# A decoder layer on one core: two data exchanges made inside SBUF, and the decay tables' sums and steps dealt anew among VectorE, TensorE and GpSimd

## The reference

```python
K = 2.0 * real(einsum('hn,hnl->hl', Ct, exp(dtA[:, :, None] * l)))   # 256 channels, 64 modes, 1024 taps
y = irfft(rfft(x, n=2048) * rfft(K, n=2048).T)[:, :1024]             # long convolution
r = x + y + x * D;  x = layernorm(x + layernorm(r) * ln_w + ln_b)
x = layernorm(x + cross_attention(x, ctx))                           # 16 heads, 77 keys
x = layernorm(x + mlp(x) + experts(x))                               # 1024 hidden, top-k of 1024 experts
```

## Time and profile before

| quantity | us |
|---|---|
| median of 3 runs | 710.08 |
| the three runs | 712.31, 710.08, 703.44 |
| the profiled execution | 702.58 |
| its span, first to last instruction | 700.8 |
| VectorE busy | 506.6 |
| TensorE busy | 590.3 |
| ScalarE busy | 404.9 |
| GpSimd busy | 279.9 |

### The profile page before, as it was taken

One profiled execution on the slowest core, in us unless ns is written; L12 is line 12 of the kernel. 1 busy time (PEld: TensorE's weight loads), 2 busy tenths in 40 slices (PEclk: granted clock), 3 DMA queues, 4 the chain that ended last, 5 costly groups with the idle time before them and its releaser, 6 DMA issues.

```text
span 700.8 us, 9712 instructions
## 1 busy us (share of the span) xinstructions
PE 590.3 (84%) x3132; PEld 383.4 (55%) x3132; DVE 506.6 (72%) x1046; ACT 404.9 (58%) x593; POOL 279.9 (40%) x333
## 2 busy tenths in 40 slices
PE   5743587785296778999999999999999999899996
PEld 2512366563264554445678565478575479453485
DVE  7999985523047885898866879767778797578783
ACT  4971655222042435797763878675579765577760
POOL 0002871635041345543343634235635234644361
PEclk9876989898596567999999999999999999999999
DMA  8945030456325000000000000000000000000000
GB/s 239 363 204 91 1 98 2 119 162 144 89 83 217 1 1 1 0 1 0 1 1 0 17 8 7 1 1 1 9 8 8 8 1 1 8 16 7 0 8 23
DMA packets 20111, 34.27 MB, mean 49 GB/s; under 512 B 7388, under 2 KB 14045, under 8 KB 18333
## 3 DMA queue, kind: packets, MB, share of 16 engines
q1 hardware_dynamic: 15677, 29.46, 13.7%
q10 hardware_dynamic: 4384, 4.20, 2.0%
HBM read 21.94 MB, written 10.65 MB: 47 GB/s over the span
## 4 chain that ended last, share of the span: by engine, by line
PE 60%; DVE 22%; ACT 7%; issue 6%; POOL 3%; DMA 1%; SPq 0%; ACTq 0%; DVEq 0%; POOLq 0%
PE banks L773 20%; PE banks L863 8%; PE banks L868 7%; PE banks L818 4%; PE banks L840 3%; PE banks L795 3%; PE banks L830 3%; PE banks L804 2%; PE banks L715 2%; DVE stats L1377 2%; ACT arena L882 2%; PE banks L651 2%; DVE arena L1468 2%; PE banks L855 2%; ACT arena L1067 1%
## 5 line engine op out<-in xcount | busy, mean ns | idle before, releaser
L1169 POOL TENSOR_TENSOR arena<-arena 128x1024 f32<-128x1024 f32 x64 | 125.8, 1965 | 156.6 <-ACT arena L1067 155.6
L773 PE MATMUL banks<-arena 128*128 128x512 f32 x384 | 174.6, 596 | 5.4 <-issue 3.7
L773 PEld LDWEIGHTS banks<-arena 128*128 128x128 f32 x384 | 69.9, 190 | 83.2 <-issue 76.5
L1067 ACT ACTIVATE arena<-arena 128x1024 f32<-128x1024 f32 x64 | 73.5, 1149 | 7.5 <-DVE arena L1466 3.2
L1069 ACT ACTIVATE arena<-arena 128x1024 f32<-128x1024 f32 x64 | 73.5, 1149 | 2.1
L1468 DVE SCALAR_TENSOR_TENSOR arena<-arena 128x1024 f32<-128x1024 f32 x48 | 63.8, 1329 | 1.7
L863 PE MATMUL banks<-arena 128*128 128x256 f32 x256 | 58.4, 381 | 2.4 <-DVE tok L1504 1.2
L957 ACT COPY arena<-banks 128x512 f32<-128x512 f32 (+1 forms) x64 | 34.1, 532 | 44.8 <-PE banks L765 29.3
L868 PE MATMUL banks<-arena 128*128 128x256 f32 x256 | 57.9, 379 | 0.0
L1142 POOL TENSOR_SCALAR arena<-mv 128x1 f32<-128x1 f32 (+1 forms) x40 | 14.1, 353 | 105.2 <-DVE mv L1378 103.8
L971 ACT ACTIVATE tok<-tok,arena,rstd 128x256 f32<-128x256 f32 x48 | 27.9, 598 | 45.5 <-POOL arena L1147 44.6
(11 more groups left out here) (179 smaller groups left out, 1077.4 us busy)
## 6 DMA issues: line engine op xcount, KB each, us to landing
scr_x<-arena SPq DMA_DIRECT2D x16, 256.0 KB, 3.2
arena<-scr_x SPq DMA_DIRECT2D x2, 2048.0 KB, 13.8
arena<-scr_z SPq DMA_DIRECT2D x32, 128.0 KB
scr_z<-arena ACTq DMA_DIRECT2D x14, 256.0 KB, 7.1
tok<-in_x SPq DMA_DIRECT2D x8, 256.0 KB, 5.7
out<-tok SPq DMA_DIRECT2D x16, 128.0 KB, 1.7
arena<-in_imat SPq DMA_DIRECT2D x1, 1152.0 KB, 5.6
arena<-in_fmat SPq DMA_DIRECT2D x1, 1088.0 KB, 7.0
```

Source lines behind the costliest of these rows:

```text
L773: ins = mm(bk[:, :], w[:, k, P * m:P * m + P], src[:, k, :], start=(k == 0), stop=(k == KC - 1))
L1067: fn(ebuf[m % 2], sxb[m % 2], ACT.Prelu, bias=negt[:, n % 2, h:h + 1], alpha=FAR).then_inc(s_ranked, 1)
L1169: tt(sxb[m % 2], sim[:, n % 2, h, 0:XR].unsqueeze(2).broadcast_to((P, XR, NKEYS)), sim[:, n % 2, FH + h, :].unsqueeze(1).broadcast_to((P, ...
```

## The change

- **x**: the 16 stores go straight from `cA` to `xS`, 8 partitions each; `scr_x` and the two loads are gone. `fmat` and one row of biases are loaded earlier. All nine `x_second` come before `taps(0)`, on two pairs of banks, and their evacuations before the taps'. GpSimd's `x_bias` moves ahead of the tables.
- **z**: SyncE's queue waits for each evacuation and moves each plane from `zring` to `zB`; `scr_z`, ScalarE's stores and the loads back are gone. The ring has three slots; `inverse` uses two pairs of banks from its fifth step on.
- **Tables**: VectorE's subtraction is gone. In groups 0 to 3 and 7 TensorE accumulates v's two terms by twice as many matmuls, in groups 4 to 6 GpSimd adds them. Groups alternate between banks 0, 1 and 4, 5.
- **Small steps**: GpSimd makes both `growth` products and half of the mode weights (gains and norms), VectorE's list drops from 28 to 13 steps there. ScalarE takes the exponential first in half 0 and last in half 1, and copies keys (with bias, to `kstage`) and values out of PSUM; the value bias is a matmul. VectorE makes `kbd` only after the tables (`keys`).
- **Numbers** of `PLACE` and `LAG` for the later part shift by thousandths, which exchanges some neighbours in the order.

```diff
--- before.py
+++ after.py
-ZRING = 4
+ZRING = 3
+V_ON_POOL = (4, 5, 6)
+Z_NARROW = 4
...
-         "taps": (0.982,), "x_second": (-0.756, 0.69), "skip": (0.382,), "k_first": (5.96, 0.01, 9.6, 0.059),
-         "simw": (-1.866,), "x_bias": (2.891, 0.086), "values": (2.518,), "diagonal": (-1.627,),
-         "k_second": (7.974, 0.1, 9.65, 0.1), "spectra": (7.989999999999999, 0.1, 9.67, 0.1),
-         "inverse": (8.27, 0.1, 9.9, 0.12), "products": (0.0, 1.0, 0.0, 0.996, 0.0, 0.802, -0.084, 0.975),
...
+         "taps": (0.982,), "x_second": (-2.2, 0.237), "skip": (1.3, 0.3), "k_first": (5.99, 0.66, 9.6, 0.247),
+         "simw": (-2.4,), "x_bias": (-1.5, 0.573), "values": (3.1,), "stage": (-2.527,), "keys": (9.559,),
+         "diagonal": (-1.42,), "k_second": (8.7, 0.13, 10.05, 0.1), "spectra": (9.027, 0.13, 10.11, 0.1),
+         "inverse": (9.076, 0.13, 10.25, 0.11), "products": (0.0, 1.0, 0.0, 0.996, 0.0, 0.802, -0.084, 0.975),
...
-SCRATCH = (("scr_x", (QUAD, 2, 2, NS, NSLOT, B * D)), ("scr_z", (2, NSLOT, P, B * HC)),
-           ("scr_v", (B, HEADS, NKV, HD + 1)))
+SCRATCH = (("scr_v", (B, HEADS, NKV, HD + 1)),)
...
-    imat = imat.reshape(P, FREQ, 2, 2, NQ, NS).transpose(0, 1, 2, 3, 5, 4).reshape(P, FREQ, 2, P)
+    imat = imat.reshape(P, FREQ, 2, 2, NQ, NS).transpose(0, 1, 2, 5, 3, 4).reshape(P, FREQ, 2, P)
...
-        cross_terms = part("cross_terms", o_tab + 4096, 2, CH, HALF)
+        v_terms = [part(f"v_terms{d}", at, 2, CH, HALF) for d, at in enumerate((o_tab + 4096, o_par))]
...
+        def x_bank(m):
+
+            return 4 * (m % 2)
+
+        def group_bank(g):
+
+            return 4 * (g % 2)
+
         def z_bank(m):
 
-            return 2 * (m % 2) if m >= FREQ else 0
+            return 2 * (m % 2) if m >= Z_NARROW else 0
 
...
-            return len(range(d, upto, ZRING))
+            return sum(len(tiles_of(n % FREQ)) for n in range(d, upto, ZRING))
...
+            sp.dma_start(rows[0:1, 4, :], t["rows"][0:1, 4, :]).then_inc(s_ctx, 16)
+            sp.dma_start(fmat, t["fmat"]).then_inc(s_mat, 16)
             sp.dma_start(wqf, t["wqf"]).then_inc(s_wsim_in, 16)
             sp.dma_start(keysT, t["keysT"]).then_inc(s_wsim_in, 16)
 
             for q in range(NQ):
                 sp.wait_ge(s_xae, 2 * (q + 1))
                 for h in range(2):
-                    sp.dma_start(scr_x[q % QUAD, q // QUAD, h].rearrange("s r n -> (s r) n"),
-                                 cA[:, h, q, :]).then_inc(s_xaw, 16)
-            for dst, n in ((rows[:, :, :], "rows"), (head_mask[:, :], "head_mask"), (value_mask, "value_mask")):
+                    p0 = NS * (4 * (q % QUAD) + 2 * (q // QUAD) + h)
+                    sp.dma_start(xS[p0:p0 + NS, 0:NSLOT, :], cA[:, h, q, :]).then_inc(s_xaw, 16)
+            sp.dma_start(rows[:, 0:4, :], t["rows"][:, 0:4, :]).then_inc(s_rows, 16)
+            for dst, n in ((head_mask[:, :], "head_mask"), (value_mask, "value_mask")):
                 sp.dma_start(dst, t[n]).then_inc(s_rows, 16)
-            sp.dma_start(fmat, t["fmat"]).then_inc(s_mat, 16)
-            sp.wait_ge(s_xaw, 16 * 2 * NQ)
-            sp.wait_ge(s_cm, 4)
-            for h in range(2):
-                sp.dma_start(xS[:, 8 * h:8 * h + 8, :].rearrange("p r n -> p (r n)"),
-                             scr_x[:, :, :, :, 8 * h:8 * h + 8, :].rearrange("a b c s r n -> (a b c s) (r n)")).then_inc(
-                                 s_xb[h], 16)
             sp.wait_ge(s_kbz, 1)
             sp.dma_start(t["scr_v"].rearrange("b h k d -> k (b h) d"),
                          vaug.rearrange("k b h d -> k (b h) d")).then_inc(s_vw, 16)
...
+                sp.wait_ge(s_ze, n + 1)
+                for j, r in enumerate(tiles_of(k)):
+                    sp.dma_start(zB[NS * r:NS * r + NS, hf].rearrange("s h q n -> s (h q) n"),
+                                 zring[:, n % ZRING, j, :]).then_inc(s_zw[n % ZRING], 16)
...
-            pe.wait_ge(s_ctx, 16 * 4)
+            pe.wait_ge(s_ctx, 16 * 5)
...
+                    mm(bank[4 + b][0:NKV, D:2 * D], ctxT[:, ic, NKV * b:NKV * b + NKV], wv[:, ic, :],
+                       start=(ic == 0), stop=False)
+                if b == 0:
+                    pe.wait_ge(s_ones, 1)
+                mm(bank[4 + b][0:NKV, D:2 * D], vaug[0:1].rearrange("k b h d -> k (b h d)")[:, 0:NKV], bv[0:1],
+                   start=False, stop=True).then_inc(s_cm, 1)
...
-                if g:
-                    pe.wait_ge(s_kev, 2 * g)
+                if g >= 2:
+                    pe.wait_ge(s_kev, 2 * g - 2)
+                b0 = group_bank(g)
                 v, u = power[g % 2]
+                sums = [(c, table) for c in range(2) for table in ((v,) if g in V_ON_POOL else (v, v_terms[g % 2]))]
+                if g in V_ON_POOL:
+                    pe.wait_ge(s_vtab, V_ON_POOL.index(g) + 1)
                 for k in range(CH // 4):
                     f = slice(4 * k, 4 * k + 4)
                     for half in range(2):
                         modes = slice(64 * half, 64 * half + 64)
-                        for c in range(2):
-                            ins = mm(bank[4 + half][:, P * k:P * k + P], u[modes, c, f, :].rearrange("p f a -> p (f a)"),
-                                     v[modes, c, f, :].rearrange("p f a -> p (f a)"),
-                                     start=(c == 0), stop=(c == 1), skip_group_check=True)
+                        for j, (c, table) in enumerate(sums):
+                            ins = mm(bank[b0 + half][:, P * k:P * k + P], u[modes, c, f, :].rearrange("p f a -> p (f a)"),
+                                     table[modes, c, f, :].rearrange("p f a -> p (f a)"),
+                                     start=(j == 0), stop=(j == len(sums) - 1), skip_group_check=True)
...
-                for h in range(tiles_of(k1)[-1] // 8 + 1):
-                    pe.wait_ge(s_xb[h], 16)
-                if k1:
-                    pe.wait_ge(s_xfe, k1)
-                second_stage(k1, bank[0], bank[1], lambda r: xS[:, r, :]).then_inc(s_xf, 1)
+                pe.wait_ge(s_xaw, 16 * 2 * NQ)
+                b0 = x_bank(k1)
+                if k1 > 1:
+                    pe.wait_ge(s_xfe, k1 - 1)
+                elif k1 == 1:
+                    pe.wait_ge(s_kbz, 1)
+                second_stage(k1, bank[b0], bank[b0 + 1], lambda r: xS[:, r, :]).then_inc(s_xf, 1)
...
+                pe.wait_ge(s_kev, 2 * NGRP - 2)
                 pe.wait_ge(s_yf, m + 1)
-                if m > FREQ:
-                    pe.wait_ge(s_ze, m - 1)
-                elif m:
-                    pe.wait_ge(s_ze, m)
+                if m >= Z_NARROW:
+                    pe.wait_ge(s_tab, NGRP)
+                if m:
+                    pe.wait_ge(s_ze, m - 1 if m > Z_NARROW else m)
...
-                        pe.wait_ge(s_kbd, 1)
                         pe.wait_ge(s_kbz, 1)
+                        pe.wait_ge(s_xfe, FREQ)
...
-                for hf in range(2):
-                    pe.wait_ge(s_zr[hf], 16 * NSLOT)
+                for d in range(ZRING):
+                    pe.wait_ge(s_zw[d], 16 * z_writes(2 * FREQ, d))
...
+                if hf == 0:
+                    own.link(magnitudes())
+                    angles().then_inc(s_sin, 1)
+                else:
+                    own.link(angles())
+                    magnitudes().then_inc(s_sin, 1)
...
+                elif kind == "stage":
+
...
+                    for oc in range(KC):
+                        fn(kstage[:, oc, :], bank[4 + oc][:, 0:B * NKV], ACT.Identity,
+                           bias=pcol[:, 2 + oc:3 + oc]).then_inc(s_kst, 1)
+                        own.done(s_kst)
+                    for b in range(B):
+                        ins = nc.scalar.copy(vaug[:, b, :, 0:HD], bank[4 + b][0:NKV, D:2 * D].rearrange("p (h d) -> p h d", d=HD))
+                        if b == 0:
+                            own.link(ins)
+                        else:
+                            ins.then_inc(s_kbz, 1)
+                            own.done(s_kbz)
...
-                    act.dma_start(scr_z[hf, tiles[0]:tiles[0] + planes].rearrange("r p n -> p r n"),
-                                  zring[:, d, 0:planes]).then_inc(s_zw[d], 16)
...
+            nc.gpsimd.memset(vaug, 1.0).then_inc(s_ones, 1)
+            own.done(s_ones)
...
+            def mode_growth(hf):
+
+                pool.wait_ge(s_phase, hf + 1)
...
+                tt(growth[hf], rates[:, 0:1, f].unsqueeze(3).broadcast_to(full), st, ALU.mult).then_inc(s_growth, 1)
+                own.done(s_growth)
+
+            pool.wait_ge(s_small_ready, 1)
+            own.link(tt(norm, are, are, ALU.mult))
+            own.link(tt(spare, aim, aim, ALU.mult))
+            own.link(tt(norm, norm, spare, ALU.add))
+            nc.gpsimd.tensor_scalar(norm, norm, 0.25, None, ALU.mult).then_inc(s_norm, 1)
+            own.done(s_norm)
+            own.link(tt(gain_re, cre, are, ALU.mult))
+            own.link(tt(spare, cim, aim, ALU.mult))
```

(97 more changed lines are left out.)

94 lines of the change are left out of this document (36 added, 58 removed).

## The result

The changed kernel takes 732.38 us (median of 4 runs, 723.33 to 736.31), the kernel before, beside it on the same chip, 706.76 us (701.15 to 712.31): a ratio of 1.0347, 95% interval 1.0185 to 1.051. It is slower by 3.5%, about 26 us; the interval reaches down to 1.9%: that it is slower is clear of noise, that it is so by over 2% not quite. I had forecast 690, in a range of 669 to 718, and had given 0.17 to anything above 724. The profiled execution of the changed kernel took 731.62 us (span 729.6). Some executions of a kernel are one to two per cent slower than its others, so every ratio here is taken from the fast executions alone.

The account below looks back on a forecast made before the run. Outside TensorE's unchanged last 512.6 us, z's traffic through HBM was taken to bound, with an 18.82 us hole. Conv at 170 instead of 188.2 saves 18 us: 684.5 profiled, plus 5.5 gives 690 us, range 669 to 718.

Parts of the forecast that it names:

- parts 1 and 2: z and x each in one SBUF-to-SBUF hop at 128 GB/s: 33 us for z, 32.8 us for x.
- the row with the same destination: Profile row of the old z loads back from HBM, also writing 8 partitions: 128 GB/s, taken as the moves' rate.
- Part 2 and 3, x: x in place at 54.1 us, then all nine x_second ahead of the tables: taps(0) at 73.7, before 63.89.
- my start of 21.3: Start of the x moves, queued behind all input loads: 18.5 us plus 2.8 us for fmat.
- Part 4, tables: Subtraction gone, VectorE loses 12.5 us, groups of 4.96 us: first inverse at 123 us, before 125.9.
- Parts 1 and 5, z: First inverse to conv: z moves hidden under 42 us of spectra, plus 5 us; conv at 170 instead of 188.2.
- All three signs: Wrong if x_second waits past 65 us (or starts before 45), ScalarE waits over 5 us for slots, taps over 1 us a group for GpSimd.
- the destination is the bound: Rival, 0.14: moves into 8 partitions run near 44 GB/s, 805 us; below 77 GB/s the kernel passes 724.
- Full-speed moves: Rival, 0.19: moves run at 175 to 400 GB/s, x in place by 32 to 45 us, taps(0) about 60; 676 us.
- A compute engine takes the wait: Rival, 0.11: doubled taps at the slow clock, 7.8 us a group, or GpSimd slows; five groups, +14; 704 us.
- The rule's estimate of 771 us: x and z moves into 8 aligned partitions reach two DMA ports, 54 GB/s: 78 us each, 771 us.
- 8 engines: z loads back: DMA share 0.50 with only loads in flight, so they use 8 engines; 286/8 is 35.7 us.

Follow-up runs that it names:

- the spread moves: Changed kernel with x and z moves each writing every 4th partition of a block of 32 instead of 8 neighbours: 675.99 us, 0.9631 of the kernel before.
- x spread: Changed kernel with x moves writing every fourth partition: 699.07 us if only x moves do so, 675.99 us if z moves do too.
- K2 to K4: Move-only batches, SBUF to 8 neighbouring partitions: 1 KB pieces, planes in order; 2 KB pieces in order; planes far apart: 64, 59, 59 GB/s.
- only z spread: Changed kernel with only the z moves writing every fourth partition, x moves keeping 8 neighbours: 711.33 us, 1.0086 of the kernel before.
- z by HBM: Changed kernel with z's exchange alone taken back to scr_z in HBM, ring of three; x moves inside SBUF: 728.25 us, 1.0321 of the kernel before.
- the batch into 16 neighbours: Move-only kernel, no layer computed: 4.19 MB from SBUF in 2 KB pieces into 16 neighbouring partitions: 38.9 us, 108 GB/s.

## Why the prediction was wrong

The step that failed is the choice of one row. In parts 1 and 2 I priced a move into 8 partitions at 128 GB/s, "the row with the same destination". Measured: 69 to 74 GB/s for x, 72 and 47 for z. The profiled execution came out at 731.6 where the sum said 684.5. The 47.1 us divide so:

- **Part 2 and 3, x:** `taps(0)` at 95.9 instead of 73.7, +22.2 us. Only the rate: 4.19 MB at 74 GB/s are 56.7 us, and my start of 21.3 plus that is 78.0; x_second began at 77.3. The nine x_second then took 18.6 us; I had written 18.5 and about 1. (The terms of that 18.5 add up to 19.5, so by them `taps(0)` would stand at 74.6.)
- **Part 4, tables:** 52.1 us instead of 49.3, +2.8 us. No subtraction like that of line 1341 is left, 9.9 of the 12.7 us that I had counted on came through, and `taps` waited for GpSimd 4.3 us in two waits, over the 1 us a group that I had allowed. TensorE's clock was 0.90 there on the mean, not 1.0. 64 records took 5.01 us, not the 4.26 that I made of twice 2.13, and that at a granted clock of 1.00 (106 to 116 us): the step from 32 records to 64 was wrong, not the clock, and why, no run shows. They still fitted the 5.2 us of a group.
- **Parts 1 and 5, z:** first inverse to conv 69.1 us instead of 47, +22.1 us. With the spread moves it took 45.1: here too only the rate was off.
- **Behind conv:** 512.6 us, as forecast.

All three signs that I had named for being wrong are there: x_second waited past 65 us, ScalarE waited 38.7 us for ring slots, and taps waited for GpSimd over 1 us a group.

Of the rivals, "the destination is the bound" (0.14) named the mechanism, the side and the turning point: past 724 us below 77 GB/s. It had only the rate too low (44). With 74 GB/s its working gives x +24 and, at 69.1 us for the whole z stretch, +22: 736. "Full-speed moves" (0.19, 676 us) is what the kernel becomes once the destination is spread: 675.99, with x in place at 42.2 in its 32 to 45 and `taps(0)` at 62.2 in place of its 60. That the medians agree to the microsecond is luck: its working gives 670.5 for the profiled execution, which took 675.38. "A compute engine takes the wait" came only in those 2.8 us: of its 14 us for slow taps or GpSimd, nothing more is there once x is early (`taps(0)` to first inverse 50.4 to 52.7 us with x spread).

The sentence on the rule of the Trainium skill's "SBUF — State Buffer", section "Door 1: The DMA port swizzle", stood in the prediction, with 54 GB/s for 8 neighbours and 771 us by it, and I held against it. The rule gives the rate of one group of partitions, and 59 to 61 GB/s was measured for it. The 128 were of a stream of loads to different groups, which I had written down as a condition ("unless successive transfers spread over different ports") without asking whether the new moves meet it. They do not: K2 to K4 run at 59 to 64 GB/s in any order. The rule's estimate of 771 us was too high since the moves ran faster in the kernel, at 69 to 74 GB/s for x. This rate wandered between executions with the same moves: from 40 to 50 us it was 74 GB/s in the changed kernel, 81 with only z spread and 65 in "z by HBM", and x_second began at 77.3, 75.3 and 87.1. Why, and why the same batch by itself ran at 61, no run shows.

The second misreading was of the DMA share. "8 engines" may well be right: every batch into 8 partitions had a share of 0.46 to 0.57, both into 16 had 1.07 or 1.08. But I took the engine time of the old loads, 286 us, as work that must be done. It is time with a packet under way, and by these runs that grows where the destination is slow: the share was the same at 61, 102 and 194 GB/s, and the batch into 16 neighbours kept all engines busy at 114 GB/s:

```profile
425.00:455.00 30.00, 0.00 (x0) 0.00 (x0) 1.00 1.08 114
```
